# mLSTM gates as four column tiles with a folding matmul, and a new order of every engine, in a one-core decoder layer

## Chip, core, metric

The kernel runs on one core of a Trainium2 chip. Five engines work from queues of their own and meet at semaphores: PE (matrix products), DVE, ACT and POOL (elementwise work, each with its own strengths), SP (issues the DMAs). The metric is the device time of one execution in microseconds; lower is better.

## The reference

One decoder layer on x of 16 batches x 256 rows x 256 columns, all in float32, with a layer norm behind each of three parts. Cut to what matters:

```
x = layernorm(x + attention(x))        # 16 heads of 16, softmax over 256 keys, additive position bias
x = layernorm(x + mlstm(x, ctx, ctx))  # 4 heads of 64
x = layernorm(x + ffn(x))              # 256 -> 1024 -> 256, rows and weights quantised

# mlstm, the gates:
xc = concatenate([q, k, v], -1)        # q = x, k = v = ctx: 768 columns
ig = xc @ igate_kernel + igate_bias    # 4 columns
fg = xc @ fgate_kernel + fgate_bias    # 4 columns
cs = cumsum(log_sigmoid(fg)); log_D = cs - cs.T + ig.T, causal
D = exp(log_D - max(log_D)); C = (qk / 8) * D
h = C / (max(|sum C|, exp(-max)) + 1e-6) @ v, then normed per head
```

Since k and v are the same rows, the kernel adds their gate weights once and works with 512 columns: 256 of x1 (the output of the first norm) and 256 of the context.

## The kernel before

Batches are pipelined. Each engine has a `body(b)` that lists, by hand, its steps for one turn of the pipeline, and `iterations` runs it for b = −1 to 19. A step names its batch by a letter: n2 = b+2, n = b+1, b, c = b−1, f = b−2, e = b−3, d = b−4. The lists are in the order in which the engine executes; nothing reorders them, so a step that waits holds all behind it on its engine. Waits are on semaphores that count a producer's steps.

Attention of a batch goes head by head: `scores` (PE, L599, into banks pS0 and pS1), `biased` (DVE, L1292: adds the bias, takes the row maximum, writes sc, a ring of eight heads), `negated` (ACT L935 for one half of the rows and POOL L437 for the other: maximum minus score), `turned` (PE, L615: four 128x128 transposes into pT), `exponentials` (ACT, L947, writes pr), `values` (PE, L632: for each four heads, two sets of four column tiles of 32 columns into pO), `heads_copy` (ACT, L957). Then `heads_turned`, `attention_out`, `attention_turned` and its copy, `out_proj` (L672), the residual (DVE, L1604), the norm (`rstd` on POOL, `normed(c, 0)` on ACT), and `x1_turned` with `x1_copy`, which gives x1T.

mLSTM of batch c: the context is loaded (`load_ctx`), turned and copied (cxT). `mem_gates` makes 68 rows (4 input gates, 60 empty, 4 forget gates) x 256 in one bank from four matmuls over 128 columns each, two on cxT (L761) and two on x1T (L764). A float32 matmul shows in the trace as two instructions. `gate_rows` and `gate_logs` (ACT, L986 to L997) turn them into log gates, `forget_sums`, `input_rows`, `running_max` and `max_rows` (DVE) into cumulated sums and maxima mm. The maxima go to DRAM (`save_max`) and come back spread over all partitions (`spread_max`, tile mb, L326). `mem_late` and `mem_weights` (ACT, L966, L974) take their exponentials, `mem_causal` (POOL) masks them, `mem_weights` on DVE (L1542) multiplies with the scores of `mem_scores` (PE) into cT, `mem_values` (PE, L739 to L741) multiplies with the context, `mem_out` (ACT) copies it out. Head norm, residual and second norm follow (`normed(f, 1)`, ACT, L1036).

FFN of batch f: `row_max` and its followers (DVE) make row scales, `quantised` (ACT, L1047) and `quantised_rows` (DVE, xq) round, `rows_turned` (PE, L585 on xq) and `rows_copy` (ACT, L1064) give xqT, `gate_proj` (L693) and `up_proj` (L706) fill banks that `gate_tanh` (ACT), `gated` and `gated_up` (DVE) read; `inner_max` and followers, `scaled` (ACT, L1124) and `inner_quantised` (POOL) round the hidden rows into hq; `turn_inner` (SP, L337) transposes each half of hq by DMA into th, and `down(e, t)` (PE, L751) multiplies half t.

For the attention of later batches, `q_proj` and `k_proj` (L648) with `q_copy` and `k_copy` (ACT) feed POOL's `split_high` and `split_low` into three bf16 parts, which `load_stack` (SP, L299, six DMAs each for qs and ks) lays out for `scores`.

Three banks (pA, pB, pC) are shared by 31 uses, in the order of the table `uses`; `lease` makes PE wait until the use before in the same bank has been read.

## Time and profile before

| | us |
|---|---|
| median of 3 runs | 766.72 (765.93 to 768.02) |
| the profiled execution | 766.44 |
| its span, first to last instruction | 764.6 |
| busy in the span: PE | 640.8 (84%) |
| DVE | 617.4 (81%) |
| ACT | 597.5 (78%) |
| POOL | 483.2 (63%) |

The profile's page shows the span in 40 slices. The first six and the last four are thin (loading and preparing weights, first attention; last batch running out), and in the slices between PE, DVE and ACT are at eight or nine tenths and more at once; the granted clock of PE is 0.8 to 0.9 of full in some of the first slices and full in the middle. The mean over the span thus says less than a stretch from the middle.

### The profile page before, as it was taken

Reading aid. Unit: us, or ns where it says so; the run is one execution under the profiler, and the core shown is the slowest. Engines: PE = TensorE matmul, PEld = TensorE weight load, DVE = VectorE, ACT = ScalarE, POOL = GpSimd, SP = SyncE. Lnnn points to the kernel's source line nnn. Section 1 sums busy time; section 2 is a strip of 40 time slices with the busy share of each in tenths; the row PEclk is TensorE's granted clock in tenths of the full one; section 3 lists DMA queues with packets and bytes.
Section 4 is the critical chain, followed back from the end, with each engine's and each line's share of the span. In section 5 each row is a group of like instructions: output and inputs, shape, how many; then the busy total and the mean of one; then the engine's idle time right before and its main releaser. Section 6 shows DMA issues by size and latency. Waiting matters only on the chain.

```text
span 764.6 us, 17069 instructions
## 1 busy us (share of the span) xinstructions
PE 640.8 (84%) x4882; PEld 476.4 (62%) x4912; DVE 617.4 (81%) x2261; ACT 597.5 (78%) x1253; POOL 483.2 (63%) x833
## 2 busy tenths in 40 slices
PE   4367997999999999999999999989999989785542
PEld 3345776667676758686868676867676757452311
DVE  2755464899999999999999999988999999875752
ACT  0415795999999998989898999988999989875421
POOL 2415654667777868787778777776777765535332
PEclk8587998999999999999999999999999999897855
DMA  8887624154445545454545453635353542120201
GB/s 266 156 143 111 97 60 74 23 114 65 123 74 112 83 113 84 111 84 112 84 111 84 109 87 89 95 85 101 70 117 60 108 59 72 42 56 15 69 15 41
DMA packets 96966, 68.32 MB, mean 89 GB/s; under 512 B 40229, under 2 KB 96618, under 8 KB 96874
## 3 DMA queue, kind: packets, MB, share of 16 engines
q1 hardware_dynamic: 96874, 67.23, 44.7%
q8 instruction: 41, 0.67, 0.4%
q14 instruction: 51, 0.42, 0.2%
HBM read 29.39 MB, written 4.26 MB: 44 GB/s over the span
## 4 chain that ended last, share of the span: by engine, by line
PE 28%; DMA 23%; ACT 13%; SPq 10%; DVE 10%; issue 10%; POOL 6%; POOLq 0%; ACTq 0%; DVEq 0%
DMA mb<-mrows 13%; DMA th<-hq 7%; SPq L299 6%; PE pT L615 3%; PE pO L632 3%; ACT L997 2%; PE pA L751 2%; ACT h L1124 2%; SPq L337 2%; DVE mm L1568 2%; PE pB L739 2%; DMA ks<-parts 2%; PE pB L764 1%; PE pB L761 1%; PE pS L599 1%
## 5 line engine op out<-in xcount | busy, mean ns | idle before, releaser
L1292 DVE CUSTOM_DVE_ANT_0 sc<-pS,bias 128x256 f32<-128x256 f32 x512 | 201.4, 416 | 28.0 <-PE pS L599 26.8
L947 ACT ACTIVATE pr<-pT 128x512 f32<-128x512 f32 x256 | 154.5, 608 | 22.0 <-PE pT L615 21.4
L615 PE MATMUL pT<-ident,sc 128*128 128x128 f32 x1024 | 153.1, 277 | 5.1 <-POOL sc L437 3.2
L437 POOL TENSOR_SCALAR sc<-sc,mx 128x256 f32<-128x256 f32 x256 | 123.3, 493 | 23.3 <-DVE mx L1292 20.8
L615 PEld LDWEIGHTS pT<-ident,sc 128*128 128x128 f32 x1024 | 119.6, 142 | 28.1 <-issue 17.1
L935 ACT ACTIVATE sc<-sc,mx 128x256 f32<-128x256 f32 x256 | 130.2, 516 | 3.0 <-DVE mx L1292 3.0
L599 PE MATMUL pS<-ks,qs 96*128 96x256 bf16 x512 | 93.8, 274 | 9.1 <-DVE mx L1292 6.5
L489 POOL TENSOR_SCALAR_AFFINE_SELECT mb<-mb 128x256 f32<-128x256 f32 x64 | 26.3, 411 | 80.2 <-ACT mb L974 79.2
L632 PE MATMUL pO<-pr,va 128*32 128x256 f32 x1024 | 70.2, 393 | 0.5 <-ACT pr L947 0.5
L599 PEld LDWEIGHTS pS<-ks,qs 96*128 96x128 bf16 x512 | 47.9, 98 | 34.0 <-DVE mx L1292 17.0
L449 POOL TENSOR_SCALAR hq<-h 128x512 bf16<-128x512 f32 x64 | 38.7, 620 | 32.0 <-ACT h L1124 31.8
L414 POOL TENSOR_SCALAR parts<-qk_f 128x512 bf16<-128x512 f32 x32 | 19.9, 621 | 56.0 <-ACT qk_f L1092 39.1
L751 PE MATMUL pA<-wd,th 128*128 128x256 bf16 x256 | 37.4, 295 | 19.4 <-DMA th<-hq 17.8
L1036 ACT ACTIVATE x<-y,shift,rs 128x256 f32<-128x256 f32 x64 | 34.7, 592 | 20.3 <-POOL shift L402 20.3
L632 PEld LDWEIGHTS pO<-pr,va 128*32 128x32 f32 x1024 | 27.1, 110 | 29.8 <-issue 9.7
L1488 DVE TENSOR_TENSOR h<-h,pA 128x512 f32<-128x512 f32 x64 | 43.7, 683 | 1.1 <-PE pA L706 0.7
L1304 DVE BATCH_NORM_STATS2 st<-y 128x6 f32<-128x256 f32 x96 | 36.0, 417 | 9.4 <-POOL y L505 9.3
L751 PEld LDWEIGHTS pA<-wd,th 128*128 128x128 bf16 x256 | 25.4, 104 | 28.9 <-issue 22.6
L1124 ACT ACTIVATE h<-h,magic,hs 128x1024 f32<-128x1024 f32 x32 | 39.5, 1236 | 4.6 <-DVE hs L1521 4.6
L391 POOL TENSOR_SCALAR ve<-mv 128x2 f32<-128x2 f32 x48 | 12.2, 254 | 48.7 <-DVE mv L1314 48.5
L416 POOL TENSOR_TENSOR qk_f<-qk_f,parts 128x512 f32<-128x512 f32 x32 | 41.2, 1287 | 2.7
L1292 DVE DVE_READ_ACCUMULATOR2_ANT mx<- 128x1 f32 x512 | 41.5, 81 | 0.0
(223 smaller groups left out, 1736.3 us busy)
## 6 DMA issues: line engine op xcount, KB each, us to landing
qs<-parts SPq DMA_DIRECT2D x96, 128.0 KB, 4.7
ks<-parts SPq DMA_DIRECT2D x96, 128.0 KB, 4.5
mb<-mrows SPq DMA_DIRECT2D x16, 512.0 KB, 7.5
xin<-in_x SPq DMA_DIRECT2D x16, 256.0 KB, 2.8
bias<-in_L_attn_pos_bias SPq DMA_DIRECT2D x4, 1024.0 KB, 20.8
xb<-in_x SPq DMA_DIRECT2D x16, 256.0 KB, 3.0
cx<-in_ctx SPq DMA_DIRECT2D x32, 128.0 KB, 2.1
out<-hq SPq DMA_DIRECT2D x16, 256.0 KB, 3.2
```

Of the source, the lines that this page charges most:

```text
L299: sp.dma_start(dst, src).then_inc(stack.sem, 16)
L416: pool.tensor_tensor(src, src, parts[:, 0, which, :, :], ALU.subtract).then_inc(split.sem, 1)
L437: pool.tensor_scalar(sc[:, s % RING, 1, :], sc[:, s % RING, 1, :], -1.0, mx[:, s % RING, 1:2], ALU.mult, ALU.add).then_inc(neg_g.sem, 1)
L599: ins = pe.matmul(pS[s % 2][:, t * S:t * S + S], qs[par][:, s, t * P:t * P + P], ks[par][:, s, :], start=True, stop=True)
L615: ins = pe.transpose(bank[:, kt * S + t * P:kt * S + t * P + P], sc[:, s % RING, t, kt * P:kt * P + P], ident[:])
L632: ins = pe.matmul(pO[32 * j:32 * j + 32, 0:S], va[par][:, kt, hd, :], pr[:, hd % RING, kt, :], start=(kt == 0), stop=(kt == TT - 1))
L751: ins = pe.matmul(bank[:, 0:D], hqT[:, t, j, :], wd[:, j, :], start=(j == 0), stop=(j == FT - 1))
L935: act.activation(sc[:, s % RING, 0, :], sc[:, s % RING, 0, :], ACT.Identity, bias=mx[:, s % RING, 0:1], scale=-1.0).then_inc(neg_a.sem, 1)
L947: act.activation(flat(pr[:, s % RING, :, :]), pT[s % 2][:, :], ACT.Exp, scale=-1.0)\
L1124: act.activation(h[:, t, :], h[:, t, :], ACT.Identity, bias=magic[:, :], scale=hs[:, 4, t:t + 1])\
L1292: dve.tensor_tensor_reduce(out=sc[:, s % RING, t, :], in0=pS[s % 2][:, t * S:t * S + S], in1=bias[:, t, s, ::-1], scale=1.0, scalar=LOW, o ...
L1488: dve.tensor_tensor(dst, dst, bank_of(f"u{i}")[:, :], ALU.mult).then_inc(h_v.sem, 1)
```

## The change

Two things are changed.

The gates. The four matmuls over 128 columns each no longer add up in one bank region. The weights are now packed in 32 columns (4 input, 4 forget, 24 zero) and the four matmuls write four different groups of 32 partitions of one bank (`gate_parts`). ACT copies the bank to gt, which now has 128 partitions (`gate_copy`), and one matmul with a matrix of zeros and ones, `fold`, adds the four groups and puts the forget gates at partition 64 again (`gate_sums`). What follows is as before. `fold` is made in the setup by two small reductions over the identity matrix, and POOL clears it.

The orders. Each engine's `body` is listed anew, with the table `uses` of the shared banks (32 uses, since the gates have two). The words of the change say that the FFN is one batch nearer; in the lists the letters d and e give way to e and f in several places. Since the point at which each list begins has moved too, the place of a step among its neighbours is what counts.

```
-        gate_w = sb("gate_w", [P, 6, 64 + XH])
+        gate_w = sb("gate_w", [P, 6, 32])
+        fold = sb("fold", [P, 64 + XH])
-        gt = sb("gt", [64 + XH, S])
+        gt = sb("gt", [P, S])
...
-            ("y1", 3, y_v, 2), ("gates", 1, gt_a, 3), ("q", -2, q_f, 1), ("xqT", 2, xq_sb, 1), ("k", -2, k_f, 1),
+            ("xT", -2, xT_sb, 1), ("v", -1, v_sb, 1), ("x1T", 1, x1T_sb, 1), ("y1", 3, y_v, 2), ("gp", 1, gp_sb, 1),
+            ("gates", 1, gt_a, 1), ("q", -2, q_f, 1), ("k", -2, k_f, 1), ("xqT", 2, xq_sb, 1), ("g0", 2, h_v, 1),
...
-            def mem_gates(c):
+            def gate_parts(c):
+
+                if not live(c):
+                    return
+                bank = lease(pe, "gp", c)
+                pe.wait_ge(cxT_sb.sem, cxT_sb.at(c, 1))
+                pe.wait_ge(x1T_sb.sem, x1T_sb.at(c, 1))
+                for j in range(4):
+                    rows = cxT if j < KT else x1T
+                    ins = pe.matmul(bank[32 * j:32 * j + 32, 0:S], gate_w[:, 2 + j if j < KT else j - KT, :],
+                                    rows[:, j % KT, :], start=True, stop=True)
+                ins.then_inc(gp_ps.sem, 1)
+
+            def gate_sums(c):
 
                 if not live(c):
                     return
                 bank = lease(pe, "gates", c)
-                pe.wait_ge(cxT_sb.sem, cxT_sb.at(c, 1))
-                for kt in range(KT):
-                    pe.matmul(bank[0:64 + XH, 0:S], gate_w[:, 2 + kt, :], cxT[:, kt, :], start=(kt == 0), stop=False)
-                pe.wait_ge(x1T_sb.sem, x1T_sb.at(c, 1))
-                for kt in range(KT):
-                    ins = pe.matmul(bank[0:64 + XH, 0:S], gate_w[:, kt, :], x1T[:, kt, :], start=False,
-                                    stop=(kt == KT - 1))
-                ins.then_inc(gt_ps.sem, 1)
+                pe.wait_ge(gp_sb.sem, gp_sb.at(c, 1))
+                pe.matmul(bank[0:64 + XH, 0:S], fold[:, :], gt[:, :], start=True, stop=True).then_inc(gt_ps.sem, 1)
...
+            def gate_copy(c):
+
+                if not live(c):
+                    return
+                act.wait_ge(gp_ps.sem, gp_ps.at(c, 1))
+                wait(act, gt_v, c - 1, 2)
+                act.activation(gt[:, :], bank_of("gp")[:, 0:S], ACT.Copy).then_inc(gp_sb.sem, 1)
...
+            for part in range(2):
+                step(dve.tensor_reduce(fold[:, 64 * part:64 * part + XH],
+                                       ident[:, :].rearrange("p (j c) -> p c j", j=4)[:, XH * part:XH * part + XH, :],
+                                       AX.X, ALU.add))
```

POOL's list shows how the steps of one engine have moved:

```
-                split_low(n, 1)
-                negated(b, 1)
...
                 split_high(n2, 0)
                 split_low(n2, 0)
-                split_high(n2, 1)
-                residual_in(b)
+                negated(b, 14)
                 negated(b, 15)
                 negated(n, 0)
+                split_high(n2, 1)
+                mem_causal(c, 0)
+                mem_causal(c, 1)
+                negated(n, 1)
+                negated(n, 2)
+                mem_causal(c, 2)
+                mem_causal(c, 3)
+                negated(n, 3)
+                inner_quantised(f, 0)
+                negated(n, 4)
+                inner_quantised(f, 1)
+                split_low(n2, 1)
```

SP in the steady part, before: the store of an output (out), the two context loads (cx), the first hidden transpose (th), the ks loads, the second transpose.

```order
L342 DMA out<-hq 128x2x256
L312 DMA cx<-in_ctx 128x256 x2
L337 DMA_TRANSPOSE th<-hq 128x8x128
L299 DMA ks<-parts 16x8x512 x6
L337 DMA_TRANSPOSE th<-hq 128x8x128
L319 DMA mrows<-mm 4x256
L305 DMA xin<-in_x 128x2x256
L331 DMA xb<-in_x 128x2x256
L326 DMA mb<-mrows 128x4x256
```

After:

```order
L344 DMA out<-hq 128x2x256
L339 DMA_TRANSPOSE th<-hq 128x8x128
L314 DMA cx<-in_ctx 128x256 x2
L339 DMA_TRANSPOSE th<-hq 128x8x128
L301 DMA ks<-parts 16x8x512 x6
L333 DMA xb<-in_x 128x2x256
L321 DMA mrows<-mm 4x256
L307 DMA xin<-in_x 128x2x256
L328 DMA mb<-mrows 128x4x256
```

Both transposes now stand ahead of the ks loads, with the context loads between them, and the load of the residual rows (xb) has left the space between the loads of xin and mb.

PE from the gates to the first gate projection, before. The banks' names stand on the left; pS is `scores`, pT `turned`, gate_w the gates, wqT and wkT the q and k projections, ident_b with xq is `rows_turned`, wg with xqT `gate_proj`.

```order
L615 MATMUL pT<-ident,sc 128x128 x4
L761 MATMUL pB<-cxT,gate_w 68x256 x2
L764 MATMUL pB<-x1T,gate_w 68x256 x2
L599 MATMUL pS<-ks,qs 128x256 x4
L648 MATMUL pC<-xT,wqT 128x256 x4
L599 MATMUL pS<-ks,qs 128x256 x2
L615 MATMUL pT<-ident,sc 128x128 x8
L585 MATMUL pA<-ident_b,xq 128x128 x4
L648 MATMUL pB<-xT,wkT 128x256 x4
L599 MATMUL pS<-ks,qs 128x256 x4
L693 MATMUL pC<-wg,xqT 128x512 x2
```

After, from the transposes behind `gate_parts` on; gt with fold is the new folding matmul:

```order
L618 MATMUL pT<-ident,sc 128x128 x4
L776 MATMUL pB<-gt,fold 68x256
L602 MATMUL pS<-ks,qs 128x256 x2
L618 MATMUL pT<-ident,sc 128x128 x4
L602 MATMUL pS<-ks,qs 128x256 x2
L651 MATMUL pC<-xT,wqT 128x256 x4
L602 MATMUL pS<-ks,qs 128x256 x2
L651 MATMUL pA<-xT,wkT 128x256 x4
L602 MATMUL pS<-ks,qs 128x256 x2
L618 MATMUL pT<-ident,sc 128x128 x4
L635 MATMUL pO<-pr,va 32x256 x8
L588 MATMUL pB<-ident_b,xq 128x128 x4
```

The k projection has moved from behind `rows_turned` to ahead of it, and so have the first value matmuls (pO); a transpose group stands between the parts and the fold.

ACT from the gate rows on, before. Rows with gate_b and gate_nb are `gate_rows`, att is `quantised`, the first table load belongs to the logarithm (sp behind it), qk_f is `q_copy` and `k_copy`, xqT `rows_copy`, pr `exponentials`, th `gate_tanh`.

```order
L986 ACTIVATE sp<-pB,gate_b 4x256
L987 ACTIVATE gt<-pB,gate_b 4x256
L988 ACTIVATE gt<-pB,gate_nb 4x256
L990 ACTIVATE sp<-sp 4x256
L1047 ACTIVATE att<-x,magic,fs 128x256 x2
L997 ACT_TABLE_LOAD
L997 ACTIVATE sp<-sp 4x256
L1092 ACTIVATE qk_f<-pC,bqk 128x256 x2
L1064 ACTIVATE xqT<-pA 128x512
L947 ACT_TABLE_LOAD
L947 ACTIVATE pr<-pT 128x512
```

After; the pair x<-y is `normed(f, 1)`, which stood ahead of the gate rows before:

```order
L1005 ACTIVATE sp<-pB,gate_b 4x256
L1006 ACTIVATE gt<-pB,gate_b 4x256
L1007 ACTIVATE gt<-pB,gate_nb 4x256
L1009 ACTIVATE sp<-sp 4x256
L1055 ACTIVATE x<-y,shift,rs 128x256 x2
L1016 ACT_TABLE_LOAD
L1016 ACTIVATE sp<-sp 4x256
L1111 ACTIVATE qk_f<-pC,bqk 128x256 x2
L1066 ACTIVATE att<-x,magic,fs 128x256 x2
L958 ACT_TABLE_LOAD
L958 ACTIVATE pr<-pT 128x512
L1083 ACTIVATE xqT<-pB 128x512
```

`quantised` has moved behind the logarithm and the q copy, and `rows_copy` behind a table load and one `exponentials`.

## Rows read from the trace of the kernel before

**Rows 1.** Stretch; us; busy PE, PEld, DVE, ACT, POOL; clock, DMA. First, last gate matmul.

```profile
261.60:580.30 318.70, 300.90 (x2401) 228.05 (x2416) 294.06 (x1113) 292.97 (x624) 238.66 (x409) 1.00 0.48 94
...
L761 PE MATMUL pB<-cxT,gate_w x64: 379/379/634, 101.5 to 696.6; 128*68 128x256 f32 x64
```

**Rows 2.** PE's idle time there, by what ended it: us in total, times, longest.

```profile
PE pA L739 <- DVE cT L1542: 5.7, 8, 1.3
PE pA L751 <- DMA th<-hq: 4.1, 7, 1.6
PE pB L693 <- ACT qk_f L1103: 3.7, 8, 0.5
PE pA L585 <- DVE xq L1467: 2.5, 8, 0.4
```

**Rows 3.** Chain of waits, 300 to 341: start us, us, what.

```profile
300.15 1.03 PE pA L751 x8
301.19 0.22 PE pS L599 x2
301.40 0.44 PE pT L615 x4
301.84 0.86 PE pB L761 x4
302.71 0.88 PE pB L764 x4
...
311.84 7.30 DMA mb<-mrows
...
330.24 0.59 SPq L299
...
334.17 5.09 DMA th<-hq
...
339.39 1.03 PE pA L751 x8
```

**Rows 4.** Timeline of PE, 307 to 312: start us, us, instruction [idle before].

```profile
307.32 0.38 PE L585 MATMUL pA<-ident_b,xq 128*128 128x128 bf16 x4 [0.43 <-DVE xq L1467]
307.55 1.95 PE L648 MATMUL pB<-xT,wkT 128*128 128x256 f32 x8
309.33 0.60 PE L599 MATMUL pS<-ks,qs 96*128 96x256 bf16 x4
...
310.72 1.07 PE L632 MATMUL pO<-pr,va 128*32 128x256 f32 x16
311.73 0.65 PE L615 MATMUL pT<-ident,sc 128*128 128x128 f32 x4
```

**Rows 5.** Timeline of PE's weight loader at the same `values` step.

```profile
310.72 0.59 PEld L632 LDWEIGHTS pO<-pr,va 128*32 128x32 f32 x16 [0.42 <-issue]
```

**Rows 6.** Timeline of ACT, 300 to 309.

```profile
300.51 0.37 ACT L957 ACTIVATE oT<-pO 128x256 f32<-128x256 f32 x1
300.81 0.51 ACT L935 ACTIVATE sc<-sc,mx 128x256 f32<-128x256 f32 x1
...
305.38 1.09 ACT L1047 ACTIVATE att<-x,magic,fs 128x256 f32<-128x256 f32 x2
306.50 1.28 ACT L997 ACT_TABLE_LOAD   x1
...
308.23 0.84 ACT L1092 ACTIVATE qk_f<-pC,bqk 128x256 f32<-128x256 f32 x2
308.96 0.60 ACT L1064 ACTIVATE xqT<-pA 128x512 bf16<-128x512 bf16 x1
```

**Rows 7.** Tile th: first hidden transpose (issued 328.89), issue to landing.

```profile
DMA to landing us min/median/max: 3.2/3.2/3.2
```

**Rows 8.** Timeline of the start: POOL at 63, DVE's small add in the setup.

```profile
63.05 2.79 POOL L437 TENSOR_SCALAR sc<-sc,mx 128x256 f32<-128x256 f32 x6
...
10.00 0.30 DVE L1237 TENSOR_TENSOR gate_w<-gate_w 128x136 f32<-128x136 f32 x1
```

More of the change, by code:

```diff
@@ L832, in body @@
                 n2, n, c, f, e = b + 2, b + 1, b - 1, b - 2, b - 3
[L833 to L841 removed]
+                scores(b, 6, par)
                 mem_values(f, 2)
@@ L866, in body @@
-                scores(b, 11, par)
-                down(e, 1)
+                gate_sums(c)
                 scores(b, 12, par)
                 turned(b, 7)
-                mem_gates(c)
                 scores(b, 13, par)
+                q_proj(n2)
                 scores(b, 14, par)
-                q_proj(n2)
+                k_proj(n2)
                 scores(b, 15, par)
                 turned(b, 8)
+                values(b, 0, par)
+                rows_turned(f)
+                scores(n, 0, 1 - par)
@@ L1142, in body @@
[L1142 to L1155 removed]
+                n2, n, c, f = b + 2, b + 1, b - 1, b - 2
@@ new lines, in body @@
+                mem_late(c, 2)
+                mem_weights(c, 2)
+                exponentials(b, 14)
+                exponentials(b, 15)
+                mem_out(c, 0)
+                heads_copy(b, 2)
+                mem_late(c, 3)
+                mem_weights(c, 3)
+                scaled(f, 0)
+                heads_copy(b, 3)
+                mem_out(c, 1)
+                negated(n, 0)
+                negated(n, 1)
+                mem_out(c, 2)
+                scaled(f, 1)
+                mem_out(c, 3)
```

273 lines of the change are left out of this document (124 added, 149 removed).

## The prediction

> **What bounds the kernel now.** I read four views in this order. First, the busy times of one long steady stretch, from the gate matmuls of one batch to those of the batch eight later. They are 318.70 us, so 39.84 us per batch; PE is busy 300.90 us, which is 37.6 per batch, DVE 36.8, ACT 36.6, POOL 29.8 [rows 1]. Three engines are nearly full; PE is the fullest and still idles 2.2 us per batch. Its clock is at full grant (1.00) there, so no clock term enters the steady part.
>
> Second, what ends PE's idle time in that stretch [rows 2]: the first mLSTM value matmul on DVE's cT 5.7 us in 8 batches (0.71 each), `down` on the transposed hidden rows 0.51, the second gate projection on ACT's k copy 0.46, `rows_turned` on the quantised rows 0.31.
>
> Third, the chain of waits over one batch [rows 3]. It closes on itself: `down(e, 1)` at 300.15, a score, a transpose group, the four gate matmuls, (logs and running max), the spread of the maxima by DMA (7.30 us), the mLSTM part, `scaled`, a hidden transpose issued by SP, six ks loads issued between it and the second one, the second transpose (5.09 us), and `down(e, 1)` again at 339.39. It is 39.24 us round, which is the distance of this batch: this loop and a nearly full PE set the pace together. A change has to shorten both.
>
> Fourth, two rows of the start [rows 8], below.
>
> **The change part by part.** All prices per batch, in the steady part, unless said.
>
> Gates. Removed: four matmuls of 256 columns, 0.86 + 0.88 = 1.74 us on PE [rows 3]. Added: one set of four column tiles and one folding matmul. The trace has such a set: `values` is two sets in one row, starting 310.72 and followed by the next transpose at 311.73, so 0.50 each [rows 4]. The fold is one matmul of 256 columns, half of 0.86, 0.43. Net −0.81 on PE. ACT gains one copy from PSUM of 128x256; its twin `heads_copy` starts at 300.51 and the next instruction at 300.81, so 0.30 [rows 6]. Between set and fold stands one transpose group of 0.44 on PE [rows 3], which covers the copy and its handoffs if ACT is free. If ACT is not free it costs up to one instruction, 0.5; below nothing is excluded, since the fold cannot start before the set ends. I take 0.15.
>
> How a switch of tile shape costs: PE's transposes start 1.01 us after the 16 instructions of the two sets, and the engine shows no gap in front of them (the projection before ends as they begin), though weight loading stood idle 0.42 us [rows 4, 5]. The Trainium skill, "TensorEngine Tiling (Array Packing)", Key Properties, says that changing the tiling mode drains TensorE, which speaks against this change: it adds a switch into column tiles and one out. If each drain cost the 0.42 of the loader, the two would eat 0.84 and the gate edit would be worth nothing on PE; by the matmul rows it costs under 0.1. I go by the rows.
>
> Hidden transposes on SP. Before, six ks loads stand between the two; now only the context load does, and `scaled(f, 1)` stands before the last mLSTM copy, where two exponentials and the attention copy used to be ahead of it. The second transpose took 5.09 us behind the ks loads [rows 3], the first, with only the context load ahead of it, 3.2 [rows 7]. With six issues of about 0.65 also gone, it lands 4 us or more earlier against the mLSTM part. `down(e, 1)` itself stands some 2 us earlier. So its wait goes: −0.51, and the loop above gets shorter than PE's own work. What is next in that loop is the running max: it now comes behind `normed`, the logs, `q_copy`, `quantised` and `quantised_rows`, about 1.8 us later after the gate rows than before, while ACT has about 2.1 us more to do before it wants the maxima. I take the wait for the maxima as unchanged.
>
> k copy. `k_proj` moves from behind `rows_turned` to ahead of it and its bank is wanted only by `up_proj(f, 0)`, much later than its copy: −0.46.
>
> What is lost: the quantised rows. Put the end of the gate matmuls at 0, where ACT starts the gate rows. Before, that was 303.59, `quantised` started 1.8 later (305.38) and `rows_turned` 3.7 later, with PE idle 0.43 in front [rows 3, 4, 6]. Now ACT does the gate rows (1.8), `normed` (two instructions of `quantised`'s kind and shape, so 1.1), table load and logs (306.50 to 308.23, 1.73), `q_copy` (0.73), then `quantised` 1.1, ending at 6.4; the handoff over DVE took 0.85 (306.47 to 307.32), so `rows_turned` starts no earlier than 7.3. PE has until there four scores (0.22), two transpose groups (0.44), two projections (1.78 each, 307.55 to 309.33) and one `values` (1.00) [rows 3, 4]: 6.3. It idles 1.0 where it idled 0.31. Then `rows_copy` stands behind a table load and an exponential, so it ends about 8.85, and PE has 0.23 + 0.22 + 0.44 of work after 7.3: 0.65 idle, with `k_proj` no longer there as filler. Together +1.3. From below, the term is 0 if ACT runs ahead by then; from above 2.2, if ACT comes to the gate rows an exponential and a `normed` late.
>
> cT. The value matmul now stands 3.6 us behind the transposes of head 13 on PE (before 4.1), while ACT does one `sc` sign flip less ahead of the maxima and the three first pairs of exponentials stand together. I take 0.35 of the 0.71 as gone; 0 and 0.71 are the ends.
>
> Sum on PE: −0.81 + 0.15 − 0.51 − 0.46 + 1.3 − 0.35 = **−0.7 per batch**. PE's own time would be 39.1, with 36.8 busy. ACT then has 36.9 busy and 2.2 idle, DVE 36.8 and 2.3; both must get by with less idle than their 3.2 and 3.0 of now, which is possible because much of ACT's is waiting for PE. The ends of the terms give −2.0 and +0.9.
>
> It counts for about 14 batch distances: the gate matmuls run from 101.5 to 696.6 [rows 1], 15 distances, and in the last PE is already short of work. −9.8 us.
>
> Start. In the fill POOL's sign flip of head 1 waited until 63.05 behind two split steps [rows 8]; now flips 0 to 4 of batch 0 stand ahead of `split_low` of the k part, about 1.8 us earlier, of which the first transposes see perhaps 1.5. The setup gets two small reductions for `fold` on DVE, on the chain there; the nearest row is the small add at 10.00, 0.30 us plus 0.04 [rows 8]; with handoffs 0.3 to 0.7. Net −1.0. End: from the last gates on (about 68 us) the chain is one batch's latency through mLSTM, norm and FFN. "One batch nearer" does not shorten it: each engine's row shows the FFN steps of a batch beside the same attention heads as before; what moved is where the loop body is cut, plus a few places. The maxima leave a little earlier, the fold copy and `scaled` ahead of `mem_out` cost a little. I take 0, ±2.
>
> Total 766.4 (the profiled execution's own time, 0.3 below the median) − 9.8 − 1.0 = **755.6, so 756**.
>
> **Rivals.** (A) PE's waits all shrink: ACT gets ahead, `rows_turned` waits as before (the 1.3 is 0.3), cT never late (−0.35 more). That is −2.0 per batch at the best and −1.65 typically: 766.4 − 23 − 1 = 742. For it: POOL and SP have room, the loop over the transposes is 3 us shorter than a batch. Against: ACT's 36.9 would have to fit in 38.2.
>
> (B) No change: the quantised rows cost 1.6 to 2.0 instead of 1.3 and cT stays late; the sum is between −0.15 and +0.1, 764 to 767. For it: three engines are within 1 us of each other, so one shortened leaves the other two; against: the chain through the transposes ran in every steady batch and is gone.
>
> (C) Slower: PE stops at `rows_turned`. Everything behind it waits, the scores of the next batch first, and DVE, which has only those to work on, next. From the point at which ACT starts the gate rows 1 us after the fold ended, the term is 2.3 to 2.5 instead of 1.3; with cT and copy at their bad ends the batch is 0.9 longer: 766.4 + 12.6 − 1 = 778. For it: `exponentials(b, 6)` stands between copy and gate rows; against: PE's transposes of head 6 end just as ACT gets there.
>
> (D) ScalarE becomes the bound: if it keeps its 3.2 us of waiting and has 0.30 more to do [rows 1, 6], the batch is 40.14 and the total 766.4 + 4.2 − 1 = 770. The Trainium skill, "TensorEngine Tiling (Array Packing)", PSUM Bottleneck, states this rule: tiling speeds TensorE up and not the evacuation of PSUM. The trace agrees in so far as the copy is of the size of half of what PE saves.
>
> **How the numbers follow.** Forecast (751 to 762) 0.50, A 0.20, B 0.14, C 0.09, D 0.07. Likeliest time 756. Faster by over 0.3% (2.3 us, about what a measurement here can tell): 0.72, forecast, A and a sliver of B; within 0.3%: 0.13; slower: 0.15. The range takes the forecast, half of A, B and D: 742 to 770.
>
> **What would show it.** Gates: PE rows of four tiles about 0.5 per set, one fold near 0.43, a copy of 0.38 on ACT. The wait of `down` on th should be nearly gone, that of the gate projections on ACT's k copy too; the second transpose should land in about 3.2 us. The wait of `rows_turned` on xq, or of the first gate projection on xqT, should be PE's largest, 0.6 to 1.0 each per batch. In the steady stretch 39.1 us per batch. I am wrong if those waits are small (then A), if ACT's idle time stays near 3.2 (D), or if the context load, now issued between the two transposes, lands late at `ctx_turned`, which has little to spare there.

## The result: slower, and the profile after

The changed kernel takes 776.5 us (median of 14 runs, 770.9 to 779.3) against 767.0 of the kernel before in the same comparison: ratio 1.0121, 95% interval 1.0101 to 1.0141. Forecast were 756 and at most 770. The profiled execution took 776.49 us, its span is 774.8, 10.2 more than before. Here and below, a ratio leaves out executions that took over 1.5% longer than the fastest of the same kernel, while medians and spreads keep them.

First the loop. The residual behind attention on DVE comes once per batch; its first and last start of nine batches (third and last figure: how many, and when) give the batch distance.

```profile
L1629 DVE TENSOR_TENSOR y<-pC,xb x9: 682/685/690, 208.7 to 535.8; 128x512 f32<-128x512 f32 x9
```

(535.8 − 208.7) / 8 = 40.89 us. Before it was 39.84 by the gate matmuls [rows 1] and 39.86 by this row; 39.1 was forecast. The stretches of the changed kernel, with the columns of [rows 1]: eight batches, and four pieces around one quantised-rows step.

```profile
255.20:582.47 327.27, 308.03 (x2435) 227.64 (x2433) 305.31 (x1113) 297.65 (x633) 245.85 (x409) 0.96 0.52 91
...
300.00:304.00 4.00, 4.00 (x27) 3.25 (x29) 3.00 (x13) 3.92 (x8) 2.82 (x7) 1.00 0.00 0
304.00:307.00 3.00, 1.18 (x20) 0.54 (x18) 2.97 (x8) 2.97 (x5) 3.00 (x4) 1.00 0.00 0
307.00:311.00 4.00, 4.00 (x17) 1.81 (x14) 3.90 (x14) 2.89 (x7) 3.59 (x6) 0.57 0.43 126
311.00:315.00 4.00, 4.00 (x40) 2.79 (x40) 3.39 (x10) 3.83 (x11) 3.72 (x7) 1.00 0.33 99
```

PE stands mostly idle from 304 to 307, and in the 4 us behind it its granted clock is 0.57, nearly all of it at the lower of the two levels (1.2 of 2.4 GHz); it then does 17 instructions where the next 4 us hold 40. The same stretch of the seven other batches shows 0.57 to 0.63. PE loses 4 x (1 − 0.57) = 1.7 us of full-clock work per batch. Its waits in the same eight batches (as [rows 2]):

```profile
PE pB L588 <- DVE xq L1492: 14.9, 8, 2.0
PE pB L588 <- ACT x L1055: 3.0, 7, 0.5
```

The four rows of [rows 2] are down to one: cT, the hidden rows and the k copy are no longer waited for, but the quantised rows have gone from 2.5 to 14.9 us (1.86 each). PE's timeline there:

```profile
303.89 1.07 PE L635 MATMUL pO<-pr,va 128*32 128x256 f32 x16
306.78 0.38 PE L588 MATMUL pB<-ident_b,xq 128*128 128x128 bf16 x4 [1.82 <-DVE xq L1492]
307.12 0.38 PE L602 MATMUL pS<-ks,qs 96*128 96x256 bf16 x2
307.34 0.85 PE L618 MATMUL pT<-ident,sc 128*128 128x128 f32 x4
307.98 1.06 PE L696 MATMUL pC<-wg,xqT 128*128 128x512 bf16 x2
...
313.30 0.60 PE L618 MATMUL pT<-ident,sc 128*128 128x128 f32 x4
313.73 0.59 PE L696 MATMUL pB<-wg,xqT 128*128 128x512 bf16 x2
```

The same transpose group takes 0.85 behind the wait and 0.60 six us later, the same gate projection 1.06 and 0.59. Why the rows are late, in the timelines of ACT, DVE and POOL:

```profile
304.12 1.08 ACT L1066 ACTIVATE att<-x,magic,fs 128x256 f32<-128x256 f32 x2
305.22 1.28 ACT L958 ACT_TABLE_LOAD   x1
...
304.54 1.05 DVE L1481 SCALAR_TENSOR_TENSOR fs<-fs,w_gu,minus_half 128x2 f32<-128x2 f32 x1
...
305.67 0.63 DVE L1585 TENSOR_TENSOR am<-gt,cs 4x256 f32<-4x256 f32 x1
306.23 0.41 DVE L1492 TENSOR_SCALAR xq<-att 128x512 bf16<-128x512 f32 x1
...
303.94 1.63 POOL L517 TENSOR_TENSOR xb<-xb,bo_bc 128x512 f32<-128x512 f32 x1
```

ACT's `quantised` (att) ends at 305.20; DVE starts on the rows (xq) 1.03 us later. It is held up most by an instruction on 2 columns of 128 rows, the first of `row_factors`, that takes 1.05 us and ends as POOL's residual add (L517) ends, 305.59 against 305.57. (A second small factor step and `input_rows`, L1585, stand between it and the rows.) Before, the same instruction had a median of 0.24 us; the change moved the add to this place.

### The profile page after: what moved, and what is told of

It reads as the page before. It is cut to its first block, busy times and chain, and to the rows that moved or that the text cites. A ratio compares the mean times of both kernels' runs of the same rounds, so it can differ in the third digit from the quotient of the medians.

```text
span 774.8 us, 17214 instructions
## 1 busy us (share of the span) xinstructions
PE 648.9 (84%) x4944; PEld 471.4 (61%) x4944; DVE 635.8 (82%) x2263; ACT 605.7 (78%) x1269; POOL 496.0 (64%) x834
## 4 chain that ended last, share of the span: by engine, by line
PE 28%; ACT 21%; DVE 20%; issue 16%; POOL 9%; DMA 4%; SPq 2%; POOLq 0%; DVEq 0%; ACTq 0%
PE pT L618 5%; ACT pr L958 4%; DVE sc L1317 3%; ACT mb L985 3%; ACT x L1055 3%; POOL nrm L481 3%; ACT sc L946 2%; PE pB L588 2%; PE pS L602 2%; ACT th L1135 2%; PE pC L754 2%; ACT mb L977 2%; PE pC L696 2%; PE pO L635 2%; PE pA L709 2%
## 5 line engine op out<-in xcount | busy, mean ns | idle before, releaser
L1317 DVE CUSTOM_DVE_ANT_0 sc<-pS,bias 128x256 f32<-128x256 f32 x512 | 199.0, 414 | 30.3 <-PE pS L602 28.0
L958 ACT ACTIVATE pr<-pT 128x512 f32<-128x512 f32 x256 | 150.1, 593 | 17.9 <-PE pT L618 17.0
L618 PE MATMUL pT<-ident,sc 128*128 128x128 f32 x1024 | 157.8, 280 | 4.9 <-issue 3.2
L440 POOL TENSOR_SCALAR sc<-sc,mx 128x256 f32<-128x256 f32 x256 | 126.7, 504 | 9.7 <-DVE mx L1317 8.4
L946 ACT ACTIVATE sc<-sc,mx 128x256 f32<-128x256 f32 x256 | 124.3, 506 | 6.4 <-DVE mx L1317 6.2
L602 PE MATMUL pS<-ks,qs 96*128 96x256 bf16 x512 | 100.1, 283 | 6.2 <-DVE mx L1317 3.7
L1055 ACT ACTIVATE x<-y,shift,rs 128x256 f32<-128x256 f32 x64 | 35.0, 593 | 20.9 <-POOL shift L405 20.6
L1329 DVE BATCH_NORM_STATS2 st<-y 128x6 f32<-128x256 f32 x96 | 36.1, 418 | 10.2 <-POOL y L508 9.1
L588 PE MATMUL pB<-ident_b,xq 128*128 128x128 bf16 x64 | 6.7, 233 | 40.4 <-DVE xq L1492 40.4
L419 POOL TENSOR_TENSOR qk_f<-qk_f,parts 128x512 f32<-128x512 f32 x32 | 38.7, 1209 | 2.7
L430 POOL TENSOR_TENSOR parts<-qk_f,parts 128x512 bf16<-128x512 f32 x32 | 38.0, 1186 | 2.7
L1521 DVE TENSOR_REDUCE hs<-h 128x1 f32<-128x1024 f32 x32 | 38.8, 1212 | 0.1
```

Source lines behind the costliest of these rows:

```text
L419: pool.tensor_tensor(src, src, parts[:, 0, which, :, :], ALU.subtract).then_inc(split.sem, 1)
L440: pool.tensor_scalar(sc[:, s % RING, 1, :], sc[:, s % RING, 1, :], -1.0, mx[:, s % RING, 1:2], ALU.mult, ALU.add).then_inc(neg_g.sem, 1)
L602: ins = pe.matmul(pS[s % 2][:, t * S:t * S + S], qs[par][:, s, t * P:t * P + P], ks[par][:, s, :], start=True, stop=True)
L618: ins = pe.transpose(bank[:, kt * S + t * P:kt * S + t * P + P], sc[:, s % RING, t, kt * P:kt * P + P], ident[:])
L946: act.activation(sc[:, s % RING, 0, :], sc[:, s % RING, 0, :], ACT.Identity, bias=mx[:, s % RING, 0:1], scale=-1.0).then_inc(neg_a.sem, 1)
L958: act.activation(flat(pr[:, s % RING, :, :]), pT[s % 2][:, :], ACT.Exp, scale=-1.0)\
```

## Experiments

Ratios are against the kernel before on the same chip, n is the number of runs of the changed one. The distance per batch and the steady clock (that of the stretch from 255 to 582 us) are those of the one profiled execution of each run; of e5 that is the fastest of the five.

| run | n | median us | ratio, 95% | us per batch | steady clock |
|---|---|---|---|---|---|
| changed kernel | 14 | 776.5 | 1.010 to 1.014 | 40.89 | 0.96 |
| e1 quantised early | 4 | 789.5 | 1.022 to 1.032 | 42.15 | 0.95 |
| e2 idle matmuls | 5 | 761.6 | 0.987 to 0.995 | 39.79 | 1.00 |
| e3 old gates, new order | 4 | 779.9 | 1.010 to 1.019 | 40.90 | 0.98 |
| e4 new gates, old order | 4 | 779.5 | 1.010 to 1.020 | 40.76 | 1.00 |
| e5 residual add back | 5 | 761.6 | 0.980 to 0.992 | 39.18 | 1.00 |
| e6 e5 + four idle matmuls | 5 | 757.0 | 0.982 to 0.988 | 39.32 | 1.00 |
| e12 e5 + two idle matmuls | 5 | 756.2 | 0.981 to 0.989 | 39.19 | 1.00 |
| e8 e3 + four idle matmuls | 5 | 774.4 | 1.005 to 1.011 | 40.71 | 1.00 |
| e11 before + four idle matmuls | 11 | 770.9 | 1.000 to 1.006 | 39.92 | 1.00 |
| e13 e5 with old gates | 5 | 778.6 | 1.009 to 1.019 | 40.96 | 0.98 |
| e14 e5, ks loads between | 5 | 810.4 | 1.051 to 1.060 | 43.77 | 0.94 |
| e15 rows ahead of factors | 5 | 776.8 | 1.007 to 1.017 | 41.12 | 0.96 |
| e16 rows, scores, factors | 11 | 775.4 | 1.006 to 1.013 | 40.98 | 0.96 |
| e17 e12, quantised first | 5 | 757.8 | 0.979 to 0.992 | 39.49 | 1.00 |
| e7 before, transposes together | 5 | 759.8 | 0.980 to 0.994 | 39.49 | 1.00 |
| e10 e4, transposes together | 11 | 764.5 | 0.992 to 1.000 | 39.85 | 1.00 |

**Is it the clock?** Idle matmuls are put ahead of the wait for the quantised rows; they write the bank that the transposes then overwrite. The line of the bank table makes them wait until ACT has read the gates in that bank three times and not only once.

```
@@ rows_turned (PE)
-                bank = lease(pe, "xqT", f)[:, :].bitcast(BF16)
+                bank = lease(pe, "xqT", f)[:, :]
+                for k in range(4):
+                    pe.matmul(bank[:, 0:D], wqT[:, k % KT, 0:P], wkT[:, k % KT, :], start=True, stop=True)
+                bank = bank.bitcast(BF16)
@@ bank table
-            ("gates", 1, gt_a, 1)
+            ("gates", 1, gt_a, 3)
```

> The changed kernel with four matmuls of 256 columns more per batch on PE, ahead of the wait of rows_turned, into the bank that rows_turned then overwrites; they read two weight tiles and their result is not used. They take 1.74 us, where PE idles 1.9. Theory with the clock (the idle stretch makes the granted clock fall, and the matmuls behind it run at half speed, about 1.6 us lost per batch): the clock stays at 1.00 and the batch gets 1.2 to 1.6 us shorter in spite of the added work, total 752 to 762. Rival (the wait alone costs, the clock is a small matter): within 2 us of the changed kernel or slower, 775 to 780.

761.6 us. The steady stretch with its clock, and then the nine residuals, (524.8 − 206.5) / 8 = 39.79:

```profile
255.00:582.00 327.00, 317.18 (x2537) 240.46 (x2553) 309.42 (x1136) 304.85 (x646) 253.05 (x419) 1.00 0.51 92
```

```profile
L1632 DVE TENSOR_TENSOR y<-pC,xb x9: 676/685/690, 206.5 to 524.8; 128x512 f32<-128x512 f32 x9
```

Work that computes nothing takes 15 us off: with the clock kept at 1.00, the changed kernel is faster than before. The control, the same lines in the kernel before, whose clock is at 1.00 already:

> The kernel before with the same four idle matmuls ahead of its own wait for the quantised rows, as a control. Its steady clock is at 1.00 already, and the wait there is 0.31 us. Theory (idle matmuls pay only where they keep the clock up): 0.4 to 0.6 us more work per batch on PE, 773 to 777 us. Rival (they pay for another reason, as in the fill and the drain of the pipeline, where PE idles most): 758 to 764 us.

770.9 us, ratio 1.0032 (1.0005 to 1.0059): a little slower, less than the 5 us expected at least; part of the idle matmuls lies in PE's other idle time. They pay only where they keep the clock.

**Is it ScalarE's order?** `quantised` ahead of the logs on ACT, and the quantised rows ahead of the forget sums on DVE:

```
@@ scalar: body
+                normed(f, 1, par)
                 gate_rows(c)
-                normed(f, 1, par)
+                quantised(f)
                 gate_logs(c)
                 q_copy(n2)
-                quantised(f)
@@ vector: body
                 row_scale(f)
-                forget_sums(c)
                 row_factors(f)
-                input_rows(c)
                 quantised_rows(f)
+                forget_sums(c)
+                input_rows(c)
```

> The changed kernel with two moves undone: on ACT normed(f, 1) and quantised stand as before (normed ahead of the gate rows, quantised ahead of the logarithm), on DVE quantised_rows stands ahead of forget_sums. Theory (the quantised rows come late, PE idles 1.9 us per batch at rows_turned and its clock then falls to about half for 4 us): the wait falls under 0.6 us per batch, the granted clock of the steady stretch returns from 0.96 to 1.00, a batch takes 39.0 to 39.6 instead of 40.9, total 749 to 760. Rival G (the new gates are what costs: the copy on ACT or the tile shapes): stays above 770. Rival W (the wait goes but comes back elsewhere, because three engines are full): 765 to 772.

789.5 us, a miss. PE's waits over eight batches:

```profile
PE pS L602 <- DVE mx L1317: 14.7, 8, 2.0
PE pT L618 <- ACT pr L958: 5.7, 8, 0.8
```

Most of the wait only changed its name: the forget sums, which wait for the later logs, now stood ahead of the biased scores of head 14 on DVE, and PE waited 1.84 us per batch for those.

**Is it POOL's residual add?** It goes back behind the sign flip of head 14.

```
@@ gpsimd: body
                 negated(b, 14)
+                residual_in(b)
                 negated(b, 15)
...
                 negated(n, 11)
-                residual_in(n)
                 negated(n, 12)
```

> The changed kernel, with one step put back: the residual add of the mLSTM input, 1.6 us on POOL, stands behind the sign flip of head 14 again and no longer beside VectorE's forget sums and row factors. Theory (POOL and VectorE collide there): forget sums 0.26 us and the two row factors 0.68 and 0.41 as before instead of 1.05, 0.95 and 0.63, so the quantised rows come about 1.0 us earlier, PE's wait for them falls from 1.86 to about 0.9 per batch, the granted clock of the 4 us behind it rises from 0.57 to 1.00, and the batch goes from 40.9 to 39.5 to 39.9: 755 to 763 us in all. Rival (the rows are late by ScalarE's order alone): the small steps stay as long or the wait stays at 1.5 or more; 773 to 777 us.

761.6 us (751.0 to 769.1; the profiled execution is the one of 751.0, the fastest). The steady stretch:

```profile
255.00:582.00 327.00, 308.07 (x2533) 230.62 (x2531) 309.24 (x1150) 307.85 (x661) 256.82 (x429) 1.00 0.52 94
```

PE's waits in it:

```profile
PE pB L588 <- DVE xq L1492: 9.3, 9, 1.2
PE pT L618 <- ACT pr L958: 5.0, 9, 0.7
```

The nine residuals, 39.18 apart, and then DVE's small factor step (minimum, median and maximum in ns):

```profile
L1629 DVE TENSOR_TENSOR y<-pC,xb x9: 682/683/685, 205.3 to 518.7; 128x512 f32<-128x512 f32 x9
...
L1481 DVE SCALAR_TENSOR_TENSOR fs<-fs,w_gu,minus_half x9: 260/260/263, 258.6 to 572.0; 128x2 f32<-128x2 f32 x9
```

The factor step is at 0.26 again, the rows' wait at 1.03 per batch, the clock full. One line on an engine that is busy for two thirds of the time is worth 15 us. (The expectation mixes up its small steps. The 1.05 is the factor step; 0.95 and 0.63 are the forget sums and the input rows, 0.69 and 0.41 before, and these two did not go back: 0.94 and 0.63 here, with POOL at its sign flips beside them.)

But the five executions spread over 18 us, and the 39.18 and the full clock are those of the fastest, 10.6 us under the median. What the clock did in the other four is not shown: of them there is no trace, and their mean clocks (0.929 to 0.940 against 0.952) don't settle it, since the profiled executions of e12 and of the kernel before have means of 0.937 and 0.933 with 1.00 in the steady stretch. Idle matmuls on top, four, and two (`range(2)` in the lines of e2):

> The changed kernel with both: the residual add put back behind the sign flip of head 14, and four idle matmuls of 256 columns ahead of the wait for the quantised rows. If the clock was the whole loss, the move adds nothing to the filler: 761 us as with the filler alone. If the lateness of the rows costs on its own too (VectorE and ScalarE then do the rest of the batch earlier), 755 to 758 us.

> The residual add put back behind the sign flip of head 14, with two idle matmuls of 256 columns ahead of the wait for the quantised rows instead of none (762 us median with a spread from 751 to 769) or four (757, 754 to 758). Theory (without them the wait of 1.0 us lies near the point at which the clock falls in part of the executions; with four, some lengthen PE's own work): 750 to 756 us, all executions within 5 us. Rival (the spread has another cause): 755 to 769 as without.

757.0 with four and 756.2 with two (754.5 to 757.2, all five executions within 3 us), at the top of the 750 to 756 expected. The spread is gone here, which fits a clock that fell in some executions of e5, but doesn't show it; e17 below has the two idle matmuls too and spreads over 8 us. What the two cost lies in the wait, 39.19 per batch against 39.18. Two are not measurably better than four. The profiled execution of e12 starts its first batch residual at 93.8 us, that of e5 at 91.3, and from the last one on it takes 79.1 instead of 76.8: most of the 5.8 us between these two executions lies outside the steady part.

**Through VectorE or through POOL?** DVE's order alone is altered, and the add stays where the change put it; `rows_turned` then waits for the fifth signal instead of the seventh.

```
@@ e15, vector: body
                 forget_sums(c)
+                quantised_rows(f)
                 row_factors(f)
                 input_rows(c)
-                quantised_rows(f)
                 biased(b, 14, 1)
```

> The changed kernel with one step moved on VectorE alone: the quantised rows stand ahead of the two row factors and of the input rows; POOL's residual add stays where the change put it. Theory (all that counts is when the quantised rows come): they come as ScalarE's quantised ends, 0.7 to 1.0 us earlier, PE's wait falls from 1.86 to 0.9 to 1.2, the granted clock behind it is 1.00, 39.2 to 39.6 per batch, 755 to 765 us. Rival (the residual add costs in that place in other ways, on POOL or by slowing the rows' own instruction): the wait stays over 1.4, 770 to 777 us.

776.8 us, a miss. Two rows of PE's timeline:

```profile
305.70 0.38 PE L588 MATMUL pB<-ident_b,xq 128*128 128x128 bf16 x4 [1.05 <-DVE xq L1492]
307.11 0.38 PE L602 MATMUL pS<-ks,qs 96*128 96x256 bf16 x2 [1.02 <-DVE mx L1317]
```

The rows came 0.8 us earlier, and the biased scores behind the factors as late as ever: 1.82 became 1.05 + 1.02. So the next one moved those scores as well.

```
@@ e16, vector: body
                 forget_sums(c)
+                quantised_rows(f)
+                biased(b, 14, 1)
                 row_factors(f)
                 input_rows(c)
-                quantised_rows(f)
-                biased(b, 14, 1)
```

> The changed kernel with VectorE's order alone altered: the quantised rows, then the biased scores of head 14, and only then the two row factors and the input rows; POOL's residual add stays where the change put it. In the run with the rows alone moved ahead the waits of PE only changed places (1.05 us for the rows and 1.02 us for the scores' maxima), so POOL's add could still cost in two ways. Theory (VectorE's lateness is all that counts): both waits shrink together, to 1.0 to 1.3 us per batch, the granted clock stays at 1.00, 39.2 to 39.7 per batch, 753 to 765 us. Rival (the sign flips of heads 12 and 13, which stand 1.6 us later on POOL behind the add, count too, or other work of VectorE does): the waits or the batch stay, 40.5 or more, 770 to 777 us.

775.4 us, the time of the rival. PE's timeline:

```profile
310.44 0.38 PE L588 MATMUL pB<-ident_b,xq 128*128 128x128 bf16 x4 [1.06 <-DVE xq L1492]
310.78 0.38 PE L602 MATMUL pS<-ks,qs 96*128 96x256 bf16 x2
311.69 0.63 PE L618 MATMUL pT<-ident,sc 128*128 128x128 f32 x4 [0.53 <-ACT pr L958]
312.18 0.59 PE L696 MATMUL pC<-wg,xqT 128*128 128x512 bf16 x2
312.90 0.61 PE L602 MATMUL pS<-ks,qs 96*128 96x256 bf16 x2
```

The stretches around them, with the clock:

```profile
309.00:311.00 2.00, 0.94 (x14) 0.37 (x6) 1.33 (x5) 1.97 (x4) 2.00 (x3) 1.00 0.00 0
311.00:313.00 2.00, 1.34 (x9) 0.65 (x8) 1.94 (x8) 2.00 (x6) 1.67 (x5) 0.93 0.00 1
313.00:315.00 2.00, 2.00 (x6) 0.63 (x5) 1.97 (x8) 1.10 (x3) 1.92 (x3) 0.50 0.51 142
```

The two waits are those of e5 (1.04 and 0.55 in its profiled execution), so VectorE's lateness does explain them. But the steps put off make the next maxima late: DVE ends one at 312.84, and PE's next scores start at 312.90, 0.72 us behind the projection, where e5 has 0.43 (301.03 to 301.46). The clock then falls to 0.50, and it stays at 1.00 in the profiled execution of e5. That these 0.3 us more make the difference is likely and not shown. So the add costs through VectorE, and no order of VectorE's steps tried here gets round it. Whether the sign flips behind the add have a share was not separated.

**What is the gate edit worth?** The old four matmuls in place of `gate_parts`, and neither `gate_copy` nor `gate_sums`: in the changed order (e3), with idle matmuls (e8), and with the residual add back (e13).

```
@@ e3, tensor: body
-                gate_parts(c)
+                mem_gates(c)
...
-                gate_sums(c)
```

> The new order with the gates as before: four accumulating matmuls where gate_parts stood, no copy, no fold. Theory (the order costs, the new gates help): PE has 0.8 us more per batch ahead of the gate rows, so these and the quantised rows come later: 0.3 to 0.8 us more per batch, 780 to 788. Rival G (new gates cost): 764 to 772.

> The changed order with the four old gate matmuls and with the four idle matmuls ahead of the wait for the quantised rows: beside the filler run it gives the worth of the column tiles at full clock. Theory (PE sets the pace once its clock is full): the old gates cost 0.5 to 0.8 us per batch, 769 to 773 us. Rival (ScalarE, VectorE or the loop over them sets it): 761 to 763 us. In both the granted clock of the steady stretch is 1.00.

> The changed order with the residual add put back, but with the four old gate matmuls in place of the column tiles, the copy and the fold: the worth of the gate edit alone, in an order in which the clock is full. Theory (it saves 0.66 to 0.9 us per batch on the path, as predicted and as the two filler runs differ): batch distance 39.9 to 40.1 against 39.18, 770 to 775 us. Rival (the saved time only lengthens the wait for the quantised rows): 761 to 764 us.

779.9, 774.4 and 778.6; e8 and e13 came out above the 769 to 773 and 770 to 775 expected. At full clock: 40.71 (e8) against 39.79 (e2), 0.92 us per batch. In e13 the batches come in two kinds, 40.1 to 40.2 and 41.6 to 41.8 us, almost in turn. The stretch behind the same step in one of each:

```profile
309.00:313.00 4.00, 3.27 (x30) 1.64 (x31) 3.78 (x16) 3.99 (x9) 3.63 (x6) 1.00 0.33 107
350.50:354.50 4.00, 4.00 (x20) 2.13 (x24) 2.72 (x11) 2.75 (x7) 3.63 (x5) 0.59 0.54 150
```

In both PE had waited 1.48 and 1.47 us for the rows and then 0.73 for an exponential; the clock fell in the second and not in the first. That prices one fall at 1.5 us in this order, and the gate edit at 40.2 − 39.18 = 1.0.

Per batch, e3 and the changed kernel look alike, 40.90 and 40.89, but they are not at the same clock. In e3 PE waits 2.3 us per batch for the rows, longer than in the changed kernel, and yet its clock falls in every third batch only. Its wait over eight batches, a batch with a fall and one without:

```profile
PE pB L588 <- DVE xq L1483: 18.6, 8, 2.4
```

```profile
303.00:344.00 41.00, 37.72 (x299) 29.31 (x300) 37.68 (x139) 36.38 (x78) 30.17 (x51) 0.96 0.52 91
344.00:385.00 41.00, 37.61 (x303) 28.80 (x305) 37.57 (x139) 36.98 (x80) 30.88 (x52) 1.00 0.53 91
```

A batch of e3 takes 41.5 us with a fall and 40.7 without, the 40.71 of e8. So the 0.92 us that the edit saves are there in the changed kernel too; they are eaten because its clock falls in every batch, which costs it 40.89 − 39.79 = 1.1 us against e2. And the length of one wait does not say by itself whether the clock falls.

The gates alone in the order of before (parts and fold in one bank, the copy ahead of `exponentials(b, 7)`):

```
@@ e4, tensor: body
+                gate_parts(c)
                 turned(b, 7)
-                mem_gates(c)
+                gate_sums(c)
@@ e4, scalar: body
+                gate_copy(c)
                 exponentials(b, 7)
```

> The order of before with the new gates alone: gate_parts ahead of the transposes of head 7, gate_copy ahead of exponentials 7, gate_sums where the gates stood; parts and fold share one bank, so that the bank table stays. Theory: 0.8 us less on PE per batch, of which the loop over the transposes lets through 0.3 to 0.7: 756 to 763. Rival G: 768 to 775. Rival W (nothing comes of it): 764 to 768.

779.5 us, 11 slower than the kernel before on the same chip (768.5), a miss for the theory and for both rivals. Timelines of PE and ACT:

```profile
299.26 1.03 PE L754 MATMUL pA<-wd,th 128*128 128x256 bf16 x8 [1.10 <-DMA th<-hq]
...
301.15 0.38 ACT L994 ACTIVATE gt<-pB 128x256 f32<-128x256 f32 x1 [1.47 <-PE pB L766]
```

`down` waits for the late transpose, the parts stand behind `down`, and ACT stands in the copy behind the parts, with `exponentials`, `normed` and the gate rows behind it.

**Was the loop through the hidden transposes real?** In both directions. SP alone is altered:

```
@@ e14 (from e5), sync: body
                 load_ctx(c)
+                load_stack(n, 1 - par, 1)
                 turn_inner(e, 1)
-                load_stack(n, 1 - par, 1)
@@ e7 (from before), sync: body
-                turn_inner(d, 1)
...
                 turn_inner(e, 0)
+                turn_inner(e, 1)
                 load_stack(n, 1 - par, 1)
```

> The changed kernel with the residual add put back, and the six ks loads between the two hidden transposes again, as before: the loop of the prediction. Theory (the loop through the transposes set part of the pace): the second transpose lands 4 us or more later, PE waits at down for the transposed rows, batch distance 39.6 to 40.2, 767 to 776 us. Rival (with scaled earlier there is slack for it): no wait at down, 39.2 per batch, 755 to 763 us.

810.4 us, 43.77 us per batch, far more than expected. The chain of waits closes on itself again, as in [rows 3], with the split of the k part on POOL (parts) ahead of the ks loads now:

```profile
337.51 1.17 POOL parts L430
338.70 0.58 SPq L301
...
342.63 5.29 DMA th<-hq
```

And PE's wait for it, over eight batches:

```profile
PE pC L754 <- DMA th<-hq: 16.9, 8, 2.4
```

That is 2.1 us per batch. Its steady clock is 0.94 where that of e5 is 1.00, so a part of the 4.6 us per batch is the clock's; the two were not separated.

> The kernel before with one step moved on SP alone: the second hidden transpose ahead of the six ks loads. Theory (the loop of the prediction sets part of the pace there): PE's wait at down for the transposed rows (0.56 us per batch) goes, batch distance 39.3 to 39.5 against 39.86, 758 to 762 us. Rival (in the old order ScalarE's scaled and POOL's quantised hidden rows come so late that SP now holds the ks loads behind them, or PE's gain is taken by the next wait): no change or slower, 764 to 772 us.

759.8 us (ratio 0.980 to 0.994), 39.49 per batch against 39.86 by the same row, as the theory had it. The second transpose still takes 5.1 us to land, with no ks load between the two; it is issued earlier (328.6 us in this trace, against 334.17 [rows 3]). PE's waits over eight batches no longer contain `down`:

```profile
PE pA L739 <- DVE cT L1542: 7.9, 7, 1.4
```

Part of the gain went to cT, 5.7 before [rows 2]. And both parts together in the old order:

> The kernel before with the new gates (779.5 us by themselves) and with the second hidden transpose ahead of the six ks loads (759.8 us by itself). Theory (the gates alone lost because ScalarE stood in their copy behind a late down(e, 1), which stood behind the late transpose): both waits go, down no longer waits for the transposed rows, 39.0 to 39.3 per batch, 750 to 758 us. Rival (the copy costs in the old order for a reason of its own, ScalarE's exponentials behind it): 40.0 per batch or more, 765 to 778 us.

764.5 us: 15 better than e4, so its loss was the transposes', but 4.7 worse than e7. PE's waits:

```profile
PE pA L742 <- DVE cT L1567: 6.7, 7, 1.4
PE pS L602 <- POOL sc L440: 3.9, 5, 0.8
PE pS L602 <- DVE mx L1317: 3.0, 4, 1.0
```

There PE waits for the spread maxima (cT) and now for flips and maxima too; its saving only lengthens waits. The theory gave 39.0 to 39.3 per batch and 750 to 758 and was wrong in that; 39.85 is near the rival's 40.0. In the old order the gates gain nothing, in the new one, at full clock, 0.92 to 1.0 us per batch.

**Is the rows' lateness all that is left?** In e12, on ACT:

```
@@ e17, scalar: body
+                quantised(f)
                 q_copy(n2)
-                quantised(f)
```

> The fastest order so far (residual add put back, two idle matmuls) with ScalarE's quantised ahead of its q copy, 0.73 us. Theory (PE's two waits here, for the rows and for the exponentials behind the table load, share one chain on ScalarE: gate rows, table load, logs, q copy, quantised, table load, exponential): the rows come 0.7 us earlier, but the exponential doesn't, so the wait only moves to it; 39.0 to 39.3 per batch, 753 to 758 us. Rival (the rows' lateness is the whole wait): 38.6 to 38.9 per batch, 745 to 751 us.

757.8 us, in the theory's range; the 39.49 per batch is above its 39.0 to 39.3, in a profiled execution that is the slowest of five (761.7). PE's largest wait over eight batches:

```profile
PE pT L618 <- ACT pr L961: 7.1, 8, 1.1
```

The wait for the exponential grew from 4.6 us (nine waits in e12) to 7.1 (eight here); the rows' was covered already. What is left is the length of ACT's chain with two table loads.

## Why the prediction was wrong, step by step

*Gates, −0.81 + 0.15.* Right in kind; on PE a little less came, in the whole batch more. The changed kernel's rows are those asked for, a set, the transposes over it and the fold, with the copy in between:

```profile
296.89 0.41 PE L766 MATMUL pA<-cxT,gate_w 128*32 128x256 f32 x2
...
297.46 0.66 PE L618 MATMUL pT<-ident,sc 128*128 128x128 f32 x4
298.12 0.62 PE L776 MATMUL pB<-gt,fold 128*68 128x256 f32 x2
```

From the first part to the transposes it is 0.57 us (0.50 predicted), from the fold to the next scores (298.58) 0.46. The transposes between take 0.66 up to the fold where 0.44 is usual, so the copy costs 0.2 (0.15 taken). And `down`, ahead of the set, takes 0.98 us (from 295.91) where it takes 0.89 ahead of the old gates in e13 (297.87 to 298.76), in each of eight batches: 0.09 for the switch into the column tiles. The Trainium skill ("TensorEngine Tiling (Array Packing)", Key Properties) names a drain at a change of tiling mode. The trace agrees in so far as this switch costs something, and its size is under the 0.1 that the prediction allowed. On the way out a drain can't be told from the 0.2 of the copy. From `down` to the scores behind the gates it is 2.67 us against 3.11 in e13 (297.87 to 300.98): PE saves 0.44, where 0.66 was predicted. The rest of the 0.92 to 1.0 us that the edit saved at full clock came from the waits, as ACT reaches the gate rows earlier: 1.03 and 0.55 us in e5 against 1.48 and 0.73 in e13.

*Hidden transposes, −0.51.* Right: the second lands in 3.1 us, and `down` waits no more. Alone it is worth 0.37 per batch (e7). What no term had is that the new order rests on it: without it, it loses 4.6 (e14).

*k copy, −0.46; cT, −0.35.* The first right. Of cT all 0.71 are gone, an end of its range.

*Quantised rows, +1.3.* This is the step that failed, in two of its parts. The first is "the handoff over DVE took 0.85". It was read where only sign flips ran on POOL; in the changed kernel it takes 1.58 (305.20 to 306.78). With the residual add moved beside it, a factor step of 0.24 takes 1.05, and `rows_turned` starts 8.0 us behind ACT's gate rows (298.78 to 306.78), where 7.3 was predicted. With the add put back it starts 7.2 behind them (292.06 to 299.27), and the idle times are 1.03 and 0.55 where the prediction had 1.0 and 0.65 (the second ended by the exponential and not by xqT). The sum of ACT's instructions was sound; what POOL does in the same microsecond was not looked at. The change of POOL's list was in the diff, and the price of that neighbourhood had no term. The Trainium skill, "SBUF — State Buffer", "SBUF: two separate sides", says that DVE instructions with two SBUF inputs and POOL instructions that read SBUF share a port pair, which the first to start keeps until it ends. The trace agrees for the factor step: it has two such inputs and ends 0.02 us behind the add. That rule should have been a rival.

The second is "no clock term enters the steady part". The clock before was full with single waits of up to 1.6 us [rows 2], but at other places of the batch. A term that puts 1.65 us of idle time close together is itself a reason to ask for the clock. It cost 1.7 us of PE's work per batch, and keeping it gave back 1.1 us per batch and 15 us in all (e2).

*The sum.* With both removed the steady part is 39.18 to 39.19 us (e5, e12), where 39.1 was predicted, and the total 756.2 (e12). That it is the forecast is partly luck: cT gave 0.36 more than was taken and the gates on PE 0.2 less, and the wait for `normed` that the changed order brought (`ACT x L1055`, 3.0 us in seven waits above, 0.4 per batch) was in no term.

*Start and end.* The first batch residual comes at 93.3 instead of 94.6 us (−1.3, predicted −1.0). That is no proof of the term: in the thirteen profiled executions with the changed order it lies between 90.4 and 94.0. The first distance after it is 35.2 instead of 39.2, a gain not predicted. The end is 77.1 us against 77.3 (predicted 0). With 604.4 us between the first and the last residual against 592.8 the parts add up: −1.3 + 11.6 − 0.2 = 10.1, of 10.2.

*Slips in the working.* With the low ends of its terms the sum goes to −2.3 and below, not −2.0. And by its own conditions rival B gives −0.03 to +0.37 per batch, 765 to 771 us, not 764 to 767; neither changes the account.

*Rivals.* C, "PE stops at `rows_turned`", gave 778 and is what happened in place and size, at a chance of 0.09; but its mechanism was ACT coming late to the gate rows, which it did not (298.78, 0.2 behind the fold). D: ACT did not become the bound: its busy share fell from 0.92 of the stretch [rows 1] to 0.91, and in e5 it idles 2.3 us per batch, where the forecast had 2.2.

## What to carry to other kernels

When an order is set anew, price each moved step also by what runs beside it in its new place: on POOL above all, a large add beside DVE's smallest instructions can stretch the one that everything waits for. When a term of the sum puts new idle time on PE, add a rival in which the granted clock falls behind it, and measure idle matmuls in that wait: here they paid where the clock had fallen (e2) and not where it was full (e11). Before two batch distances are compared, compare their clocks (e3). A saving on an engine shows only where that engine, and not a loop through DMAs, sets the pace; here the place of one DMA issue among six others was worth 8 us in one order (e7) and 49 in the other (e14 against e5, the clock's part included).

## What the runs showed of the hardware

- PE idle for 1.82 us between two instructions, behind full work: in the 4 us behind it the granted clock was 0.57 to 0.63, in each of eight batches. With 1.05 and 1.02 us, 0.4 apart, it fell as well (e15, steady clock 0.96). With 1.04 and 0.55 it stayed at 1.00 over the whole steady stretch of one execution (e5, profiled). With 2.3 us it fell in three of eight batches (e3).
- So the same waits can give either clock (e13, e3). The Trainium skill, "TensorE: Matmul & The Clock Gate", Part 1, says that the gate's window runs free of the program; falls in every second batch (e13) and in every third (e3) agree with it.
- A 128x2 instruction of DVE took 1.05 us beside POOL's 128x512 add and 0.26 without it; the add itself took 1.63 instead of 1.28.
- A switch from full-width matmuls to four column tiles took 0.09 us more of PE than none (0.98 against 0.89 us for `down`, e13).
- The second hidden transpose landed in 5.1 us (before) and 5.3 us (e14) behind six ks loads, and in 3.1 us in the changed kernel behind the context loads. But it took 5.1 us in e7 too, straight behind the first transpose, so what lengthens it is not isolated.
